# Feed-forward weights loaded and made ternary in the block of loads, ahead of attention, instead of ahead of the feed-forward stage

## The reference

```python
x = x + tanh(g_xattn[0]) * attention(layernorm(x), ctx, ctx)          # 16 heads of 16, no weights
x = x + tanh(g_ffn[0])   * ffn(layernorm(x), w1, conv_w, conv_b, w2)  # below
x = x + tanh(g_xattn[1]) * projected_attention(layernorm(x), ctx, ctx, Wq, Wk, Wv)
x = x + tanh(g_ffn[1])   * experts(layernorm(x), ...)                 # 8 experts, top 2

def act_quant(x):    s = 127 / clip(max|x| over the last axis, 1e-5);  return clip(round(x * s), -128, 127) / s
def weight_quant(w): s = 1 / clip(mean|w|, 1e-5);                      return clip(round(w * s), -1, 1) / s
# ffn: w1 is 1024 x 256, w2 256 x 1024
h = act_quant(x) @ weight_quant(w1).T
h = silu(depthwise convolution of h over the tokens, 3 taps, + conv_b)
return act_quant(h) @ weight_quant(w2).T
```

## Time and profile before

| | us |
|---|---|
| median of three runs | 1912.14 (1907.1, 1912.14, 1913.4) |
| profiled execution, its own time | 1907.65 |
| its span, first to last instruction | 1905.9 |
| block of loads to attention's first instruction | 0 to 37.5 |
| attention, layer 0 | 37.5 to 368.8 |
| deviation and preparation | 369.6 to 395.5 |
| feed-forward block, first centring | 397.3 |
| its first product | 410.4 |

### The profile page before, as it was taken

The page is one execution under the profiler, slowest core; times in us unless marked ns, Lnnn a source line. Parts: engine busy times, 40 slices in busy tenths (PEclk is TensorE's granted clock), DMA queues, the critical chain, the costliest instruction groups (busy, mean ns, idle before and its releaser), DMA issues. The chain is left out here.

```text
span 1905.9 us, 52438 instructions
## 1 busy us (share of the span) xinstructions
PE 1607.3 (84%) x20058; PEld 1099.5 (58%) x20058; DVE 1580.5 (83%) x2986; ACT 1183.2 (62%) x1912; POOL 861.8 (45%) x930
## 2 busy tenths in 40 slices
PE   1899999536777667756999999997899999999998
PEld 0777777424444444434777777775565565566565
DVE  6899999757888988876888888886888888888885
ACT  2799999558777787725888888886333232333332
POOL 1455555216777777772333333332233333333332
PEclk9999999869988999877999999998899999999999
DMA  9100000100000000000002000000121221211212
GB/s 318 37 3 3 3 3 3 46 0 1 1 0 0 0 0 0 0 5 14 3 3 69 2 2 2 2 2 2 46 101 68 82 84 55 100 66 61 98 63 67
DMA packets 45470, 67.43 MB, mean 35 GB/s; under 512 B 6272, under 2 KB 36736, under 8 KB 45312
## 3 DMA queue, kind: packets, MB, share of 16 engines
q1 hardware_dynamic: 45024, 65.05, 10.1%
q10 hardware_dynamic: 288, 0.00, 0.0%
HBM read 56.39 MB, written 8.65 MB: 34 GB/s over the span
## 5 line engine op out<-in xcount | busy, mean ns | idle before, releaser
L638 ACT ACTIVATE a_exp<-a_score_t 128x1024 f32<-128x1024 f32 x256 | 262.5, 1025 | 83.3 <-PE a_score_t L448 82.6
L563 DVE TENSOR_REDUCE a_maxes<-a_score 128x8 f32<-128x1024 f32 x256 | 310.8, 1214 | 0.6 <-PE a_score L431 0.6
L1529 POOL TENSOR_TENSOR e_a_parts<-e_act,e_a_parts 128x512 f16<-128x512 f32 x128 | 153.4, 1198 | 332.2 <-ACT e_a_parts L1500 332.2
L1500 ACT ACTIVATE e_a_parts<-e_act 128x512 f16<-128x512 f32 x128 | 80.6, 630 | 313.7 <-DVE e_act L1332 308.9
L1077 POOL TENSOR_TENSOR b_hidden<-b_hidden,b_shifted 128x508 f32<-128x508 f32 x128 | 161.8, 1264 | 152.2 <-DVE b_hidden L930 151.9
L1214 PE MATMUL e_up_ps<-e_n_turned,e_up_t 128*128 128x512 f16 x768 | 187.9, 381 | 9.7 <-DVE e_act L1328 9.7
L1228 PE MATMUL e_out<-e_down_t,e_a_parts 128*128 128x256 f16 x1536 | 188.4, 273 | 0.8 <-POOL e_a_parts L1529 0.8
L1214 PE MATMUL e_gate<-e_n_turned,e_gate_t 128*128 128x512 f16 x768 | 187.9, 381 | 0.2 <-issue 0.2
L1228 PEld LDWEIGHTS e_out<-e_down_t,e_a_parts 128*128 128x128 f16 x1536 | 149.6, 98 | 39.0 <-POOL e_a_parts L1529 1.1
L1084 POOL TENSOR_TENSOR b_hidden<-b_hidden,b_scales 128x512 f32<-128x512 f32 x128 | 168.3, 1319 | 3.1 <-ACT b_scales L1059 3.1
L867 PE MATMUL b_hid<-b_x_turned,b_w1t 128*128 128x512 f16 x512 | 143.3, 406 | 27.3 <-DVE b_hidden L930 24.1
(11 more groups left out here) (204 smaller groups left out, 4042.6 us busy)
## 6 DMA issues: line engine op xcount, KB each, us to landing
ctx<-e_weights SPq DMA_DIRECT2D x64, 512.0 KB, 5.5
out<-x SPq DMA_DIRECT2D x16, 512.0 KB, 2.9
x<-in_x SPq DMA_DIRECT2D x3, 2048.0 KB, 16.7
ctx<-in_ctx SPq DMA_DIRECT2D x1, 4096.0 KB, 26.8
ctx<-in_ctx SPq DMA_DIRECT2D x1, 3072.0 KB, 16.4
b_raw<-in_L_ffn_w SPq DMA_DIRECT2D x2, 1024.0 KB, 7.1
x<-in_x SPq DMA_DIRECT2D x1, 1536.0 KB, 16.4
ctx<-in_ctx SPq DMA_DIRECT2D x1, 1024.0 KB, 13.4
```

The source lines that it names most:

```text
L563: nc.vector.tensor_reduce(maxes[:, p * PAIRS:(p + 1) * PAIRS], score[:, :].rearrange("p (h k) -> p h k", k=P), AX.X, ALU.max).then_inc(max ...
L638: nc.scalar.activation(exp32[:, u % 2, 2 * p:2 * p + 2, :], score_t[:, :].rearrange("p (g n) -> p g n", g=2), ACT.Exp, scale=DH ** -0.5 / ...
L1529: nc.gpsimd.tensor_tensor(a_parts[:, e % 4, 1, :], act3[:, e % 2, :], a_parts[:, e % 4, 0, :], ALU.subtract).then_inc(alo_ok, 1)
```

## The change

- SP issues w1 and w2 ahead of all of x. The taps and conv_b are issued by ScalarE's queue, behind the gates.
- In the block of loads VectorE first fills `q_stack`, `neg_max` and `k_stack`, then does the sums, the chain, the taps, `in_back`, the gate and `out_back`, and only then x's statistics. The weights lie where attention keeps its exponentials later (`exp32`), the ternary ones in `q_turned`; the chain works in place.
- TensorE makes the total and the transposes in that block, each group into its own half of a bank pair (`score`, `score_t`), w1's when w1 is ternary, w2's when w2 is. ScalarE copies them out, ahead of its Sqrt table load.
- GpSimd clears `v_pad` and sets its ones.
- `w1t`, `w2t`, `taps`, `conv_b`, `in_back` and `out_back` are allocated ahead of attention and kept.
- The deviation block and the preparation block ahead of the feed-forward block are gone. The chain now stands at the head of the feed-forward block's VectorE program, with the factor -0.5 so that the mean has its sign turned. `magic` is filled in one column, not 512. ScalarE takes the root there and goes straight on to the centring; the Silu table load stands behind the first group's centring.

```diff
-def start_stage(nc, io, m, sem, fill_constants, make_spread):
+def start_stage(nc, io, m, sem, fill_constants, make_spread, clear_values, w):
...
+            sp.dma_start(w.raw[:, 0, :].rearrange("p (c d) -> p c d", c=HC), io["L0_ffn_w1"].rearrange("(c p) d -> p c d", p=P)).then_inc(w_in[0], 16)
+            sp.dma_start(w.raw[:, 1, :].rearrange("p (c d) -> p c d", c=DC), io["L0_ffn_w2"].rearrange("(c p) d -> p c d", p=P)).then_inc(w_in[1], 16)
             for c in range(len(x_in) - 1):
                 load_x(c)
...
+                act.dma_start(m.taps[:], io["L0_ffn_conv_w"].rearrange("(c p) a k -> p c (a k)", p=P)).then_inc(taps_in, 16)
+                act.dma_start(m.conv_b[:], io["L0_ffn_conv_b"].rearrange("(c p) -> p c", p=P)).then_inc(taps_in, 16)
             act.wait_ge(gates_in, 32)
             nc.scalar.activation(m.tanh_gates[:, :], m.gates[:, :], ACT.Tanh).then_inc(tanh_made, 1)
+            for n in range(4):
+                act.wait_ge(turned, n + 1)
+                dst = m.w1t[:, n % 2, :] if n < 2 else m.w2t[:, 4 * (n % 2):4 * (n % 2) + 4, :].rearrange("p c d -> p (c d)")
+                nc.scalar.activation(dst, w.turn[n], ACT.Copy).then_inc(copied, 1)
             nc.scalar.preload_act_table(ACT.Sqrt)
             deviation_root(nc, act, m, steps)
+            act.wait_ge(copied, 4)
...
+            pe.wait_ge(rows_ok, 2)
+            nc.tensor.matmul(w.total, m.ones32[:, 0:1].broadcast_to([P, P]), w.rows[:, :], start=True, stop=True).then_inc(total_ok, 1)
+            for n in range(4):
+                pe.wait_ge(chain, 5 if n < 2 else 8)
+                for k in range(8):
...
             make_spread(pool)
+            clear_values(pool)
...
         def _(dve):
+            fill_constants(dve)
...
+            for n in range(2):
+                dve.wait_ge(w_in[n], 16)
+                nc.vector.tensor_reduce(w.rows[:, n:n + 1], w.raw[:, n, :], AX.X, ALU.add, apply_absolute_value=True).then_inc(rows_ok, 1)
+            dve.wait_ge(rows_ok, 2)
+            dve.wait_ge(total_ok, 1)
+            then(nc.vector.tensor_scalar(w.mean[:], w.total, 1.0 / (HID * D), 1e-5, ALU.mult, ALU.max))
+            then(nc.vector.reciprocal(w.inverse[:], w.mean[:]))
+            for n in range(2):
+                then(nc.vector.tensor_scalar(w.raw[:, n, :], w.raw[:, n, :], w.inverse[:, n:n + 1], MAGIC, ALU.mult, ALU.add))
+                then(nc.vector.tensor_scalar(w.raw[:, n, :], w.raw[:, n, :], MAGIC, 1.0, ALU.subtract, ALU.min))
+                then(nc.vector.tensor_scalar(w.tern[:, n, :], w.raw[:, n, :], -1.0, None, ALU.max))
+            dve.wait_ge(taps_in, 32)
+            then(nc.vector.tensor_scalar(m.taps[:], m.taps[:], 1.0 / XS, None, ALU.mult))
+            then(nc.vector.tensor_scalar(m.in_back[:], w.mean[:, 0:1], XS, None, ALU.mult))
             fill_constants(dve, tanh_made)
+            then(nc.vector.tensor_scalar(m.out_back[:], w.mean[:, 1:2], m.tanh_gates[:, 2:3], None, ALU.mult))
             for c in range(len(x_in)):
                 dve.wait_ge(x_in[c], 16)
...
-def deviation_chain(nc, dve, m, steps):
+def deviation_chain(nc, dve, m, steps, half=0.5):
...
+            def clear_values(pool):
+                nc.gpsimd.memset(v_pad[:], 0.0).then_inc(cleared, 1)
+                pool.wait_ge(cleared, 1)
+                nc.gpsimd.memset(v_pad[:, :, :, DH:DH + 1], 1.0).then_inc(cleared, 1)
...
-            deviation_stage(nc, m, sem, "deviation", start_loads)
-            block = prep.enter_context(nc.Block())
...
             @block.vector
             def _(dve):
+                nc.vector.memset(level[:], 1.0 / 127.0).then_inc(level_ok, 1)
+                nc.vector.memset(magic[:, 0:1], MAGIC).then_inc(level_ok, 1)
+
+                deviation_chain(nc, dve, m, deviation, -0.5)
+                dve.wait_ge(level_ok, 2)
...
-                nc.scalar.preload_act_table(ACT.Silu)
+                nc.scalar.preload_act_table(ACT.Sqrt)
+                deviation_root(nc, act, m, deviation)
...
                             last.then_inc(cent_ok, 1)
+                            if isinstance(j, int) and j == 0:
+                                nc.scalar.preload_act_table(ACT.Silu)
```

More of the change, by code:

```diff
@@ L98, in start_stage @@
     counted = sem("x_counted")
+    w_in, taps_in = [sem("w1_loaded"), sem("w2_loaded")], sem("taps_loaded")
+    rows_ok, total_ok, chain, turned, copied = (sem(f"w_{n}") for n in ("rows_ok", "total_ok", "chain", "turned", "copied"))
     steps = deviation_signals(sem, "first")
@@ L394, in attention_stage @@
         else:
-            start_stage(nc, io, m, sem_scope, fill_constants, make_spread)
+            w = Shared()
+            w.raw = exp32[:].rearrange("p a g n -> p a (g n)")
+            w.tern = q_turned[:].rearrange("p (a t) n k -> p a (t n k)", a=2)
+            w.rows, w.inverse, w.mean = sb("w_rows", [P, 2], F32), sb("w_inverse", [P, 2], F32), sb("w_mean", [P, 2], F32)
+            w.total = out[:, 0:2]
+            w.turn = [b[:, n * HG * P:(n + 1) * HG * P].bitcast(F16) for b in (score, score_t) for n in range(2)]
+            cleared = sem("values_cleared")
+            def clear_values(pool):
+                nc.gpsimd.memset(v_pad[:], 0.0).then_inc(cleared, 1)
+                pool.wait_ge(cleared, 1)
+                nc.gpsimd.memset(v_pad[:, :, :, DH:DH + 1], 1.0).then_inc(cleared, 1)
+                pool.wait_ge(cleared, 2)
+            start_stage(nc, io, m, sem_scope, fill_constants, make_spread, clear_values, w)
         with nc.Block() as block:
@@ L834, in bitnet_stage @@
+        w1t, w2t, taps, conv_b, in_back, out_back = m.w1t, m.w2t, m.taps, m.conv_b, m.in_back, m.out_back
+        level = sb("level", [P, 1])
         centred = sb("centred", [P, GT, D])
@@ L848, in bitnet_stage @@
         IN, MID = 5, 3
+        deviation, level_ok = deviation_signals(sem, "deviation"), sem("level_ok")
         def chunk_behind(j, c, slots):
@@ L1560, in build_program @@
         m.expert_loaded = [sem(f"expert_loaded{n}") for n in range(4)]
-        attention_stage(nc, io, m, 0, sem)
-        m.rstd, m.mean = (v[:, :].rearrange("p (j k) -> p j k", k=GT) for v in (m.rstd2, m.mean2))
-        bitnet_stage(nc, io, m)
+        with ExitStack() as early:
+            m.w1t = early.enter_context(nc.sbuf_tensor("w1t", [P, DC, HID], F16))
+            m.w2t = early.enter_context(nc.sbuf_tensor("w2t", [P, HC, D], F16))
+            m.taps = early.enter_context(nc.sbuf_tensor("taps", [P, HC, 3], F32))
+            m.conv_b = early.enter_context(nc.sbuf_tensor("conv_b", [P, HC], F32))
+            m.in_back = early.enter_context(nc.sbuf_tensor("in_back", [P, 1], F32))
+            m.out_back = early.enter_context(nc.sbuf_tensor("out_back", [P, 1], F32))
+            attention_stage(nc, io, m, 0, sem)
+            m.rstd, m.mean = (v[:, :].rearrange("p (j k) -> p j k", k=GT) for v in (m.rstd2, m.mean2))
+            bitnet_stage(nc, io, m)
         m.rstd, m.mean = m.rstd2[:, :], m.mean2[:, :]
```

104 lines of the change are left out of this document (30 added, 74 removed).

## The result

The changed kernel took 1889.3 us (median of four, 1888.9 to 1894.23), the kernel before 1910.91 in the same comparison (1907.1 to 1913.4): a ratio of 0.990, 95% interval 0.9879 to 0.9921, that is 15 to 23 us less. The forecast was 1895.6, in a range of 1888 to 1905, and -14.3 us. A second comparison, with five and nine runs, gave 1893.34 against 1907.69: 0.9929, interval 0.9915 to 0.9942, 11 to 16 us less. Over both, the changed kernel has 9 runs with a mean of 1892.05; the kernel before has 42 (those of the second comparison and of two later ones) with a mean of 1908.15: -16.1, with some 2 us either way, an estimate from the spread of the runs. Most of what follows is about why one comparison says -21.6 and the other -14.4.

What follows compares the result with a forecast made beforehand. No single engine bounds the kernel; VectorE and loads bound the loads block, VectorE and a load the feed-forward preparation. Head -25.5 plus loads block +11.2 gave -14.3 us, from 1909.9 to 1895.6, range 1888 to 1905.

Steps and rivals of the forecast that it cites:

- The loads block: Before attention: VectorE takes on sums, chain and gate, so its statistics end at 45.8, not 34.6: +11.2 us (+9.9 to +11.8).
- the 0.6 us taken for the small packets ahead of w2: Loads block: half of the 1.2 us that 2080 small packets could delay w2, putting the second sum at 12.65.
- not +6: Loads block, rival: the loads, not VectorE, set its end, so it grows by only 6.0; 1890 us, chance 0.05.
- The small loads: Taps and conv_b on ScalarE's queue: land by 12 to 20, asked for at 23.8, so no wait for VectorE.
- The rival's pace of 45 packets per us: Loads block: 2080 small packets take 46 us, VectorE waits, +33, net +19, 1929 us; chance 0.05 for over 14 us late.
- one of handing out: Small loads: the argument that 45 packets per us was the pace of handing out packets, not of a full queue.
- The head: Feed-forward head: the first centring moves from 397.31 to 371.85, -25.5 us (-25.7 to -24.2).
- the forecast's own bound of -25.7: Feed-forward head: the largest saving allowed, with the two memsets hidden by the table load.
- Attention and the loop: Attention and later stages, code unchanged: only the timing of TensorE's clock could move them, +-4 us, taken as 0.

Runs made afterwards that it cites:

- the order of the loads: The changed kernel with x's first 2 MB loaded ahead of the weights and its 16 tiles of statistics ahead of the sums: 1896.76 us, ratio 0.9944.
- the places: The kernel before with the change's six tensors allocated, unused, ahead of attention: 1906.77 us against 1907.47, ratio 0.9995.

## Why the prediction was right, and where its sizes were off

**The loads block, +11.2 forecast, +10.5 measured.** The second sum started at 12.09, not 12.65. Of the 0.6 us taken for the small packets ahead of w2 some 0.3 is there, by the run that issues them behind w2, and without them w2 lands a little sooner than the 12.0 taken from x's first part. From the second sum to the statistics it took 12.04 (11.42 + 0.5 = 11.92 forecast), the statistics 21.00 (21.2). That from the second sum on VectorE and not the loads is the bound, which made it +10.5 and not +6, is shown by x's last part, which landed at 40.2 as forecast (39 to 40.3), by the order of the loads, and by the run with four passes on GpSimd, where VectorE was free earlier and its statistics ended 3.3 us sooner.

**The small loads, no wait forecast, none measured.** They landed at 15.3 and 19.0, within the forecast's 12 to 20, with 4.3 us in hand. That this is the weak place of the change was right as well: asked for at 15.5, they cost 3.4. The rival's pace of 45 packets per us did not hold: 2080 packets didn't take 46 us. That this pace was one of handing out was the forecast's reading, and no row shows it.

**The head, -25.5 forecast, -25.9 measured.** The memsets cost nothing, the Silu load was hidden. That is 0.2 beyond the forecast's own bound of -25.7, which let the centring start behind the root's end; it started 0.1 before it (380.79 against 380.89), and the root came 1.51 after the chain's first instruction, not 1.61. Undoing the merged block and the table load cost 2.4; so some 23.5 of the 25.9 are the moved preparation, and 2.4 the shape of the head.

**Attention and the loop, 0 with a bound of 4, measured -1.1 and -2.2 in the profile.** Both go with TensorE's clock. In attention it rose 24.1 us after the first instruction before, and 15.2 us after (with a dip of 3.4). But the run with the early wait for the taps rose after 23.7 us and took 331.2, as before, though it has the change, and two runs without the change (the places, and the kernel before with the transposes twice) rose after some 14.4 us and took 330.7 and 330.9. In the loop the low stretches differ from run to run of one kernel. So by these profiles neither difference belongs to the change.

**The sum against the medians.** The edit's own steps give 10.5 - 25.9 = -15.4 by the profile, and -15.3 by the profiles of the two kernels with the transposes twice, whose times differ by -15.7 by the ratios and -17.1 by the medians. The first comparison's -21.6 sets high draws of before (1912.14 and 1913.4, where 42 later runs have a mean of 1908.15) against low draws of after (1888.9 to 1889.4, where the other six runs lie between 1891.66 and 1895.14). The mean clock of the changed kernel over nine runs is 0.9629, of the kernel before over 42 runs 0.9562. The head alone accounts for that: the low stretch there was 44.4 us and is 20.5, and 24 us at half of full speed are 0.0063 of the span. So on average the loops ran at the same clock, and what the first comparison shows beyond -15.4 was draw. The forecast of -14.3 is 7.3 us from the first comparison and 0.1 from the second. The 0.1 is in part luck, for each comparison moves by some us with the clock of its runs; the steps, each within 0.7, are not. What sets off a low stretch in the loop was not found; that more work on TensorE nearly removes them was shown, in both kernels. That the low level is what costs the time rests on these two runs and on the slopes; another way in which the doubled transposes could shorten the loop was not tested.

## What to carry to other kernels

A preparation that only one engine works on is cheapest where that engine waits for something else; price it there by the engine's own last wait: here 12.0 us of chain cost 10.5, because 1.5 us of VectorE's waits for x went away and the first sum fell into its wait for the loads, while the old place cost some 23.5, its whole length. Before giving a pass to a second engine, try whether the two hold each other up: rounding w2 with ScalarE's help made the block 2.2 us shorter, and with GpSimd's help 9.2 us longer. And where a kernel's runs differ by more than the effect, read the effect in its stage, and compare kernels at the same granted clock.

## What the hardware showed that was not expected

- TensorE's clock is a term of the time even where TensorE isn't the bound: over 42 runs of one kernel +0.01 of its mean goes with -5.9 us. 512 more transposes in the loop, 30 to 40 us of busy time, made one kernel 7 us faster and the other 5 to 9.
- GpSimd takes 7.1 to 8.1 us for a two-operation pass over 128x2048 float32 that VectorE does in 1.23, and 5.4 for a one-operation pass; beside it VectorE's `tensor_scalar` over 128x2048 stands still until it is done (7.99 and 6.27 us, not 1.23). The statistics kept their pace (16 in 5.32), and so did three `tensor_tensor` over 128x64 with two inputs (0.26 to 0.27 each at 41.8 to 42.5 in the run with four passes, beside GpSimd's pass to 43.1).
- Small loads behind the same issue time landed 4.6 and 6.4 us later from ScalarE's queue (15.3 and 19.0) than from SP's ahead of x (10.7 and 12.5).
